# Early norm additions moved, end additions shared, and 39 matmuls into an unread bank

## The reference

```
x = x + xattn(layernorm(x), ctx)          # softmax attention to 120 context rows per batch
x = x + ffn(layernorm(x))                 # mixture of 8 experts, top 2
# ffn(h): logits = h @ Wr.T + br;  topk_w = softmax(top 2 of the logits)
#   out = sum over experts e of cw[e] * (gelu(h @ W1[e].T + b1[e]) @ W2[e].T + b2[e])
#   z = out + h;  return layernorm(z) * ln_w + ln_b      (F = 1024 hidden features)
```

## Time and profile before

| | |
|---|---|
| median of 3 runs | 643.11 us (642.44 to 644.43) |
| the profiled execution | 644.39 us, of which 642.6 us are the span of the trace |
| PE busy | 563.2 us, 88% of the span |
| DVE busy | 425.0 us (66%) |
| POOL busy | 319.7 us (50%) |
| ACT busy | 280.2 us (44%) |
| mean granted clock of PE | 0.934 of full |

### The profile page before, as it was taken

The page is one execution under the profiler, slowest core; times in us unless marked ns, Lnnn a source line. Parts: engine busy times, 40 slices in busy tenths (PEclk is TensorE's granted clock), DMA queues, the critical chain, the costliest instruction groups (busy, mean ns, idle before and its releaser), DMA issues.

```text
span 642.6 us, 17705 instructions
## 1 busy us (share of the span) xinstructions
PE 563.2 (88%) x4878; PEld 493.4 (77%) x4879; DVE 425.0 (66%) x1317; ACT 280.2 (44%) x699; POOL 319.7 (50%) x527
## 2 busy tenths in 40 slices
PE   5999999998468999998999999999999999999700
PEld 4888988887347987777989898988888898898500
DVE  2679999997844755554666666576767676576643
ACT  3688877774134233334343333324333432433113
POOL 4124334444241345453555454656766666675447
PEclk8999999996658999999999999999999999999855
DMA  7457666664430233432334243433445334344353
GB/s 230 142 155 234 211 190 202 193 209 116 149 84 18 35 50 61 64 64 51 55 61 65 55 65 58 66 75 67 77 96 90 75 75 91 67 83 81 52 147 131
DMA packets 62402, 65.70 MB, mean 102 GB/s; under 512 B 10088, under 2 KB 58032, under 8 KB 62352
## 3 DMA queue, kind: packets, MB, share of 16 engines
q1 hardware_dynamic: 46544, 44.10, 23.1%
q0 software_dynamic: 13632, 18.91, 19.0%
q10 hardware_dynamic: 2176, 2.10, 1.0%
HBM read 43.07 MB, written 22.02 MB: 101 GB/s over the span
## 4 chain that ended last, share of the span: by engine, by line
PE 41%; issue 15%; DVE 14%; POOL 14%; ACT 4%; DMA 3%; POOLq 3%; DVEq 1%; SPq 1%; ACTq 0%
PE bank L925 7%; PE bank L927 6%; PE bank L926 6%; PE bank L949 6%; PE bank L951 5%; PE bank L950 5%; POOL sums_dram L656 5%; POOL xg L637 2%; DVE st L1210 2%; DVE w2hi L1242 2%; PE bank L904 1%; POOL work L677 1%; DVE w2hi L1241 1%; POOL w1hi L721 1%; DMA sums_dram<-xn,mt 1%
## 5 line engine op out<-in xcount | busy, mean ns | idle before, releaser
L1098 ACT ACTIVATE stage<-bank,mt 128x256 f32<-128x256 f32 (+1 forms) x312 | 122.2, 453 | 141.4 <-PE bank L927 137.4
L925 PE MATMUL bank<-xnt,w1hi 128*128 128x256 f16 (+1 forms) x624 | 165.7, 267 | 9.3 <-DVE xnt L1345 5.8
L656 POOL DMA_INDIRECT sums_dram<-xn,mt x71 | 115.5, 1627 | 114.2 <-DVE xn L1369 95.7
L926 PE MATMUL bank<-xnt,w1hi 128*128 128x256 f16 (+1 forms) x624 | 165.0, 266 | 0.0
L927 PE MATMUL bank<-xnt,w1lo 128*128 128x256 f16 (+1 forms) x624 | 164.8, 266 | 0.0
L949 PE MATMUL bank<-w2hi,stage 128*128 x552 | 150.6, 273 | 3.9 <-DVE xn L1364 3.7
L951 PE MATMUL bank<-w2hi,stage 128*128 x552 | 150.5, 273 | 0.0
L950 PE MATMUL bank<-w2lo,stage 128*128 x552 | 150.5, 273 | 0.0
L1354 DVE CAST stage<-stage 128x512 f16<-128x512 f32 (+1 forms) x156 | 64.3, 412 | 111.8 <-PE bank L951 103.9
L1356 DVE TENSOR_TENSOR stage<-stage 128x512 f16<-128x512 f32 (+1 forms) x156 | 102.6, 658 | 5.4
L637 POOL DMA_INDIRECT xg<-tokens_dram,mt x71 | 74.7, 1052 | 51.7 <-POOL mt L632 26.7
(11 more groups left out here) (225 smaller groups left out, 917.6 us busy)
## 6 DMA issues: line engine op xcount, KB each, us to landing
stage<-in_L_ffn_W_dram SPq DMA_DIRECT2D x16, 768.0 KB, 5.0
work<-in_L_ffn_b_dram SPq DMA_DIRECT2D x39, 128.0 KB, 3.0
x<-in_x_dram SPq DMA_DIRECT2D x16, 256.0 KB, 4.8
tokens_dram<-xn SPq DMA_DIRECT2D x16, 256.0 KB, 2.2
sums_dram<-xn SPq DMA_DIRECT2D x16, 256.0 KB, 2.7
stage<-in_L_ffn_W_dram SPq DMA_DIRECT2D x16, 256.0 KB, 3.8
work<-sums_dram SPq DMA_DIRECT2D x8, 256.0 KB, 3.4
out_dram<-x SPq DMA_DIRECT2D x8, 256.0 KB, 3.2
```

What stands on the lines that cost most here:

```text
L656: nc.gpsimd.indirect_dma_start(out=sums_dram, out_offset=bass.IndirectOffsetOnAxis(ap=sidx[p][:, t:t + 1], axis=0), in_=y_sb[p][:, t, :], ...
L925: nc.tensor.matmul(dst, w1hi[:, col], xhi[:, k, 0:bt], start=(k == 0), stop=False)
L926: nc.tensor.matmul(dst, w1hi[:, col], xlo[:, k, 0:bt], start=False, stop=False)
L1098: ins = nc.scalar.activation(h32[:, c * bt:(c + 1) * bt], f_h[q][:, (c % 2) * bt:(c % 2 + 1) * bt], ACT.Gelu, bias=b1s[p][:, c:c + 1], sca ...
```

## The change

Six things change.

1. PE gets 39 matmuls that write bank 3, which nobody reads before it is written again (`spin`): 16 after the matmul for the table's keys, 10 after the one for the list, 7 after late group 3, 6 after `turn(0, 0)`. They read finished weights and wait for nothing.
2. In `up(0, 0)` late group 4 is turned after the second quarter, `turn(0, 1)` runs after the third, group 5 after the fourth, and groups 6 and 7 after `up(0, 0)`. ACT and DVE take the parts in that order, with the high and low part of block 1's rows between groups 5 and 6.
3. In `down` of a short block the `turn` stands at c == 2.
4. When block 11 (the first full one after the short ones) is split, `x_low` of block 12 goes first; before it went after the second quarter.
5. `finish_early(i)` moves behind `y_out(m, 1)`; for i = 7 both the multiplication by ln_w (from POOL to DVE) and the addition move behind the last block's `y_out`, and its store moves in SP's queue behind the loads of the sums.
6. At the end POOL adds batches 8 to 12 and DVE 13 to 15; `norm_pair(2)` comes before POOL's first addition and `norm_pair(3)` before its second; ACT's stores wait accordingly.

```diff
+            def spin(n):
+                for _ in range(n):
+                    nc.tensor.matmul(bank[3][:, 0:BT], w1hi[:, 0:P], w1hi[:, 0:BT], start=True, stop=True)
...
                              start=True, stop=True).then_inc(table_mm, 1)
+            spin(16)
             pe.wait_ge(table_ready, 3)
...
+            spin(10)
             late_groups(transpose_group, 1, 4)
             pe.wait_ge(blocks_ready, 1)
+            spin(7)
...
-                    if c == KF // 2 and turned is not None:
+                    if c == (KF // 2 if tiles(m, p) == TB else KF // 4) and turned is not None:
                         turn(*turned)
...
             turn(0, 0)
             pe.wait_ge(wlo_ready, GROUPS * NB + 4 * LATE - 8)
-            up(0, 0, weights_at(0, 0), (0, 1), beside=lambda q: late_groups(transpose_group, 4 + q, 5 + q))
-            turn(0, 1)
+            spin(6)
+            def beside(q):
+                if q == 2:
+                    turn(0, 1)
+                elif q > 0:
+                    late_groups(transpose_group, 4 + q // 2, 5 + q // 2)
+            up(0, 0, weights_at(0, 0), (0, 1), beside)
+            late_groups(transpose_group, 6, 8)
...
# ACT
             for q in range(HB):
                 gelu(0, 0, q)
-                late_groups(high_part, 4 + q, 5 + q)
+                if q == 1 or q == 2:
+                    late_groups(high_part, 3 + q, 4 + q)
             x_high(0, 1)
+            late_groups(high_part, 6, 8)
...
             def store(b):
-                if b < NB - 1:
+                if b < ON_TIME + HANDED:
                     act.wait_ge(o_ready, b - ON_TIME + 1)
                 else:
-                    act.wait_ge(last_done, 1)
+                    act.wait_ge(last_done, b - ON_TIME - HANDED + 1)
...
# DVE
             def ahead(m1, p1, m2, p2):
+                if isinstance(m1, int) and 2 * m1 + p1 == FIRST + SHORT:
+                    x_low(m2, p2)
+                    split(m1, p1)
+                    return
...
-                if i is not None:
+                y_out(m, 1)
+                if i is not None and i < ON_TIME - 1:
                     finish_early(i)
-                y_out(m, 1)
...
-            late_groups(low_part, 4, 8)
+            late_groups(low_part, 4, 6)
             x_low(0, 1)
+            late_groups(low_part, 6, 8)
...
+            dve.wait_ge(early_zn, ON_TIME)
+            z = z_now[(ON_TIME - 1) % 2]
+            nc.vector.tensor_tensor(z, z, lnw_bc[:, :].unsqueeze(1).to_broadcast([P, TJ, D]), ALU.mult).then_inc(early_zw, 1)
+            finish_early(ON_TIME - 1)
...
             measure_z(0)
             measure_z(1)
-            for q in range(2, PAIRS):
-                measure_z(q)
-                weigh(ON_TIME + 2 * q - 4)
-                weigh(ON_TIME + 2 * q - 3)
-            for b in range(NB - 4, NB):
+            measure_z(2)
+            weigh(ON_TIME)
+            weigh(ON_TIME + 1)
+            measure_z(3)
+            for b in range(ON_TIME + 2, ON_TIME + HANDED + 1):
                 weigh(b)
+            for b in range(ON_TIME + HANDED, NB):
+                finish(b)
+                if b + 1 < NB:
+                    weigh(b + 1)
...
# POOL
-            weigh_early(ON_TIME - 1)
...
             norm_pair(0)
             norm_pair(1)
-            for q in range(2, PAIRS):
-                norm_pair(q)
-                finish(ON_TIME + 2 * q - 4)
-                finish(ON_TIME + 2 * q - 3)
-            for b in range(NB - 4, NB - 1):
+            norm_pair(2)
+            finish(ON_TIME)
+            norm_pair(3)
+            for b in range(ON_TIME + 1, ON_TIME + HANDED):
                 finish(b)
...
# SP
-                if p == 1 and 0 <= m - ON_TIME_AT < ON_TIME:
+                if p == 1 and 0 <= m - ON_TIME_AT < ON_TIME - 1:
                     store_early(m - ON_TIME_AT)
...
                 sp.dma_start(z_all[:, b, :, :], sums_v[:, b, :, :]).then_inc(sums_loaded[b % 4], 16)
+            store_early(ON_TIME - 1)
```

More of the change, by code:

```diff
@@ L70, in build @@
     ON_TIME_AT = 11
+    HANDED = 5
     UNITS = E * PER_EXPERT + E * TB
@@ L1459, in weigh, with finish @@
                                         lnw_bc[:, :].unsqueeze(1).to_broadcast([P, TJ, D]), ALU.mult).then_inc(zw_ready, 1)
+            def finish(b):
+                dve.wait_ge(zw_ready, b - ON_TIME + 1)
+                nc.vector.tensor_tensor(z_all[:, b, :, :], z_all[:, b, :, :], x1[:, b, :, :], ALU.add).then_inc(last_done, 1)
             measure_z(0)
             measure_z(1)
-            for q in range(2, PAIRS):
-                measure_z(q)
-                weigh(ON_TIME + 2 * q - 4)
-                weigh(ON_TIME + 2 * q - 3)
-            for b in range(NB - 4, NB):
+            measure_z(2)
[3 more added lines that the diff above has]
+            for b in range(ON_TIME + 2, ON_TIME + HANDED + 1):
                 weigh(b)
-            dve.wait_ge(zw_ready, NB - ON_TIME)
-            nc.vector.tensor_tensor(z_all[:, NB - 1, :, :], z_all[:, NB - 1, :, :], x1[:, NB - 1, :, :], ALU.add).then_inc(last_done, 1)
+            for b in range(ON_TIME + HANDED, NB):
+                finish(b)
+                if b + 1 < NB:
+                    weigh(b + 1)
 _INS = ['x', 'ctx_1024', 'L0_xattn_Wq', 'L0_xattn_bq', 'L0_xattn_Wk', 'L0_xattn_bk', 'L0_xattn_Wv', 'L0_xattn_bv',
```

## The result

| | median of the runs | range |
|---|---|---|
| kernel before | 642.78 us | 639.32 to 644.43 (4 runs) |
| changed kernel | 634.36 us | 632.37 to 634.98 (4 runs) |

The ratio is 0.9871, with a 95% interval of 0.9824 to 0.9917: faster by 1.3%, or 8.4 us between the medians. The forecast was 633.2 in a range of 630.5 to 637.0. Four more runs of the same kernel, in the first experiment, have a median of 631.93. The profiled execution took 634.98 us; its span fell from 642.6 to 633.3, by 9.3 us, 0.8 of which arose before anything that was changed.

What follows compares the result with a forecast made beforehand. The prediction took PE, busy 88% of the span, as the bound, with a short list of waits and low-clock stretches to remove. Terms -0.6 - 0.2 - 2.0 - 3.7 - 2.1 - 1.3 = -9.9 us gave 633.2 us, range 630.5 to 637.0.

Steps and rivals of the forecast that it cites:

- The clock at the start: At up(0, 0): the 39 added matmuls have PE's clock at 2.4 GHz when it begins, halving 5.78 us; -2.9 us.
- The new order: Before up(0, 1): the late groups' new order lengthens the chain of high and low parts behind up(0, 0); +1.7 us.
- Low clock behind the hole: After PE's hole before up(0, 1): the low-clock stretch gets longer, 4.65 in place of 3.51 us; +0.6 us.
- Short blocks: Short blocks: only the 0.2 us low-part wait ahead of block 11 goes, the seven "issue" waits stay; -0.2 us.
- Block 12: Before block 12: with the earlier turn and x_low first, PE's 2.00 us wait for the low part goes; -2.0 us.
- Early norms: In down of the early-norm pairs: y_out runs in DVE's idle time, so PE's six waits on it go; -3.7 us.
- Last pair: Last block pair: y_out comes at 599.75 instead of 601.89, a gain that carries to the end; -2.1 us.
- End: End stage: with additions shared by POOL and DVE, the last store goes out at about 637.0 instead of 638.6; -1.3 us.
- Rival 2: End stage: the additions of DVE and POOL block each other, so the end gives nothing; 634.5 us, chance 0.13.
- Rival 3: Early norms: PE's waits only change their name, the next thing being late by as much; 636.9 us, chance 0.07.
- rival 4: Pairs with early norms: POOL's L677 comes late, delaying the splits and the next down; slower, 651 us, chance 0.03.
- Rival 1: Start: the clock stays low despite the added matmuls, so the -2.9 us are lost; 636.1 us, chance 0.15.

Runs made afterwards that it cites:

- the first experiment: The changed kernel run once more with no edit; median 631.93 us (628.25 to 637.13), ratio 0.9816.
- e5_hold: The changed kernel with 26 and 12 matmuls around turn(0, 0) instead of 7 and 6, and more before up(0, 1); median 633.44 us, ratio 0.9859.
- e6_mixed: The changed kernel with the old late-group order, turn at c == 4 except in block 10, and 26, 12 and 17 matmuls near up(0, 0); median 631.65 us.
- e10_turn_all_mid: The changed kernel with the old late-group order, turn at c == 4 in block 10 too, and 17 more matmuls before up(0, 1); one time, 629.23 us.
- e7_early_only: The kernel before with only the moves of finish_early, including those for i = 7; median 635.99 us, ratio 0.9891.

## Why the prediction was right, and where it was not

The sum was -9.9 us; the profiled span gave -9.3, of which -0.8 came before the change, and the medians -8.4. That the total fell well inside the range is in part luck: errors offset one another. In the means over the traces, the matmuls gave 1.2 us less than forecast and the short blocks 1.3 less; against that the early norms gave 1.1 more, the 0.6 for more low clock did not come, and in the profiled execution 0.8 came before the change.

- **The clock at the start, -2.9.** Right in kind, too large. In the traces it is about -1.7 in the mean, an estimate from few of them. The assumption that failed is that the clock is at 2.4 GHz when `up(0, 0)` begins: in the changed kernel's first trace it was up at `turn(0, 0)`, ahead of which PE had been idle for 2.3 us, and it was at 0.50 from the first matmul of `up(0, 0)`. In other traces of the same work it stayed up. What decides it stays open.
- **The new order, +1.7.** Right to 0.1 us: 1.67, by the chain and with the 0.9 us from `wlo_ready` to the first matmul. It is a loss inside a change that gains.
- **Low clock behind the hole, +0.6.** Wrong as a difference: the low stretch there is 3.4 us with either order, or absent. It fell in six of the eight traces without matmuls in the hole, in none of the five with them.
- **Short blocks, -0.2.** This is the step that failed: I took the turn's move as free because the "issue" waits are in `up` and no turn there waits for rows. The stage lost 1.06 us in the mean, of which the turn's move costs 0.84 (0.22 remain with the turn in the middle and were not followed). I overlooked that the turn pushes back the matmuls of c == 2 and 3, on whose end DVE's next split and behind it the low part of the next rows wait. The wait ahead of block 11, which was to go, grew by 0.12 us.
- **Block 12, -2.0:** -2.16. **Early norms, -3.7:** -4.76. Both mechanisms were right and both sizes short for one reason: a matmul of 0.27 us starts 0.11 after the one before it, and the profile counts idle time from the modelled end. A wait given as 0.45 is 0.45 + 0.27 - 0.11 = 0.61 us of lost time. For the six waits that adds 6 x 0.16 = 1.0 us to 3.7; for block 12 it adds 0.16 to 2.00.
- **Last pair, -2.1:** -2.07 to -2.33 in nine of the twelve traces, with PE's wait at 2.1 as forecast. In the other three (e5_hold, e6_mixed, e10_turn_all_mid), with -1.66 to -1.77, the very last scatter started 0.5 us later; why was not followed.
- **End, -1.3:** -1.23. Against the old end in the same kernel the sharing gives 1.6 us in this trace (1.7 in the mean); the missing 0.3 is in e7_early_only too (+0.26), where the end's order is that of before. That points at the moved work or the moved store, but each of the two is a single trace, and in which of them it lies stays open. The Trainium skill's rule ("SBUF — State Buffer", Who interferes with whom: the second waits in full) is borne out in kind only: DVE's additions took 0.3 to 0.5 us more than 0.72, and none was longer by a whole POOL addition of 1.26. Rival 2 did not come.
- **Rival 3** (the waits change their name) is refuted: PE is busy 147.00 of 147.00 us over the early norms. So is **rival 4**: in none of the pairs does PE wait. **Rival 1** came in part: of the seven traces with the 39 matmuls three have low clock at the start of `up(0, 0)`, for 1.0 to 3.8 us.

## What to carry to other kernels

Price a stage by the start-to-start time of PE's matmuls, not by the listed waits: each wait hides 0.16 us more here. A step moved earlier in an in-order queue delays all that it now stands ahead of, and what other engines wait for there: here 0.22 us of transposes ahead of c == 2 and 3 held back DVE's split and, behind it, the next block. Where a hole can't be closed, filling it with matmuls into an unread bank kept the clock up in five of five traces (without, it stayed up in two of eight), but a batch that just fits at 2.4 GHz overruns at 1.2.

## What was not expected

The same kernel met different clocks at the same place: low for 2.9 us in one execution and not at all in the next at the start of `up(0, 0)`, which is 1.44 us of the time (+0.31 against -1.13). Behind the 2.0 us wait at block 12 it was low in one of two kernels that both have it, for 1.66 us. That is a part of the scatter of single executions (628.25 to 637.13 for the changed kernel); the rest was not followed. And the order of the late groups, with the same work in another order, was worth 1.67 us at one clock.
